# First tile: 64 of each sample's 528 pairs taken ahead, in eight steps of 16 samples, while the other rows are gathered

## What is computed

```python
inner = x[:, row] * x[:, col]                                   # b, 528, 128
fm = relu(einsum('bpd,ad->bpa', inner, attn_W) + attn_b)        # b, 528, 128
scores = einsum('ba,bpa->bp', gnn_feature, fm)                  # b, 528
attn = softmax(scores, axis=1)
attn_output = einsum('bp,bpd->bd', attn, inner) * 100.0         # b, 128
z = concatenate([gnn_feature, attn_output, gnn_feature], axis=1)
y = relu(relu(z @ W_top1 + b_top1) @ W_top2 + b_top2) @ W_top3
```

## Time and profile before

| | us |
|---|---|
| median of 3 runs | 1270.41 |
| the profiled execution, its own time | 1270.63 |
| its span | 1268.2 |
| TensorE busy | 1201.0 |
| VectorE busy | 1147.9 |
| ScalarE busy | 1018.7 |
| POOL busy | 451.8 |

### The profile page before, as it was taken

One profiled execution on the slowest core, in us unless ns is written; L12 is line 12 of the kernel. 1 busy time (PEld: TensorE's weight loads), 2 busy tenths in 40 slices (PEclk: granted clock), 3 DMA queues, 4 the chain that ended last, 5 costly groups with the idle time before them and its releaser, 6 DMA issues.

```text
span 1268.2 us, 20736 instructions
## 1 busy us (share of the span) xinstructions
PE 1201.0 (95%) x8732; PEld 898.7 (71%) x8732; DVE 1147.9 (91%) x649; ACT 1018.7 (80%) x1039; POOL 451.8 (36%) x270
## 2 busy tenths in 40 slices
PE   1499999999999999999999999999999999999998
PEld 1267676777777777777777777677777777777766
DVE  2399899998999989999899989999799998999994
ACT  1288898778987889878897798978888788887883
POOL 6587684018800386005840088201880000000000
PEclk9999999999999999999999999999999999999999
DMA  4211410311103111131101311031110300011001
GB/s 108 97 34 50 105 32 26 102 45 30 34 13 125 31 32 28 30 106 37 32 20 47 106 27 32 20 111 39 30 34 21 117 18 1 1 29 39 17 9 38
DMA packets 54859, 58.83 MB, mean 46 GB/s; under 512 B 10728, under 2 KB 49136, under 8 KB 53744
## 3 DMA queue, kind: packets, MB, share of 16 engines
q1 hardware_dynamic: 46304, 40.20, 10.4%
q0 software_dynamic: 8448, 17.32, 5.2%
q10 hardware_dynamic: 16, 0.00, 0.0%
HBM read 36.12 MB, written 17.31 MB: 42 GB/s over the span
## 4 chain that ended last, share of the span: by engine, by line
PE 83%; ACT 8%; issue 4%; DVE 2%; POOL 2%; another core or an unknown queue 1%; DMA 1%; SPq 0%; ACTq 0%; DVEq 0%; POOLq 0%
PE scores L610 19%; PE ring L580 17%; PE ring L587 13%; PE ring L589 12%; PE ring L588 12%; PE ring L634 4%; ACT fm L308 3%; ACT inner_hi L316 3%; PE ring L620 2%; POOL x_rows L280 2%; PE ring L654 1%; DVE products L418 1%; ACT exp_pairs L323 1%; PE ring L648 1%
## 5 line engine op out<-in xcount | busy, mean ns | idle before, releaser
L308 ACT ACTIVATE fm<-ring,attn_b_sb 128x848 f32<-128x848 f32 (+1 forms) x640 | 597.2, 971 | 183.1 <-PE ring L580 174.3
L418 DVE TENSOR_TENSOR products<-xt 128x2112 f32<-128x2112 f32 x256 | 601.9, 2351 | 37.1 <-ACT xt L347 37.1
L280 POOL DMA_INDIRECT x_rows<-in_tbl,ids_all x264 | 451.1, 1709 | 498.2 <-PE ring L620 408.3
L423 DVE TENSOR_TENSOR low_parts<-products,inner_hi 128x1688 fp32r<-128x1688 f32 (+4 forms) x256 | 467.1, 1825 | 57.1 <-ACT inner_hi L316 56.0
L587 PE MATMUL ring<-inner_hi,attn_wt_lo 128*128 128x424 f32 (+1 forms) x971 | 433.1, 446 | 5.1 <-ACT fm L308 5.1
L316 ACT CAST inner_hi<-products 128x1688 fp32r<-128x1688 f32 (+4 forms) x256 | 392.3, 1532 | 5.2 <-DVE products L418 5.2
L589 PE MATMUL ring<-inner_hi,attn_wt_hi 128*128 128x424 f32 (+1 forms) x971 | 344.1, 354 | 0.0
L588 PE MATMUL ring<-low_parts,attn_wt_hi 128*128 128x424 f32 (+1 forms) x971 | 343.7, 354 | 0.0
L580 PE MATMUL ring<-products,attn_wt 128*128 128x424 f32 (+1 forms) x618 | 275.8, 542 | 10.0 <-issue 6.4
L610 PE MATMUL scores<-fm,gnn_blocks 128*32 128x264 f32 x4096 | 254.6, 389 | 6.5 <-ACT exp_pairs L323 6.4
L587 PEld LDWEIGHTS ring<-inner_hi,attn_wt_lo 128*128 128x128 f32 x971 | 182.6, 188 | 70.8 <-issue 37.6
(11 more groups left out here) (53 smaller groups left out, 203.9 us busy)
## 6 DMA issues: line engine op xcount, KB each, us to landing
x_dram<-x_rows SPq DMA_DIRECT2D x8, 2112.0 KB, 6.6
x_fields<-x_dram SPq DMA_DIRECT2D x128, 128.0 KB
x_rows<-in_tbl,ids_all POOLq DMA_INDIRECT x264
attn_t<-attn_turned SPq DMA_DIRECT2D x124, 32.0 KB, 1.9
w_sb<-in_W_top SPq DMA_DIRECT2D x2, 512.0 KB
x_fields<-in_r_gnn_feature SPq DMA_DIRECT2D x1, 512.0 KB
h<-in_W_top SPq DMA_DIRECT2D x1, 256.0 KB
ids_all<-in_ids SPq DMA_DIRECT2D x1, 132.0 KB, 2.7
```

The source lines that it names most:

```text
L280: nc.gpsimd.indirect_dma_start(out=x_rows[:, f, :], out_offset=None, in_=tables[f], in_offset=bass.IndirectOffsetOnAxis(ap=ids_all[:, t, f ...
L308: nc.scalar.activation(dst, slot(("hidden", pair, j))[:, :, 0:n], ACT.Relu, bias=attn_b_sb[:, 0:1]).then_inc(s_fm, 1)
L418: nc.vector.tensor_tensor(dst, a, b, ALU.mult).then_inc(s_inner, 1)
L423: nc.vector.tensor_tensor(inner[:, S % INNER_BUFS, at:end], plain[:, S % INNER_BUFS, at:end], inner_hi[:, S % HI_BUFS, 0:end - at].bitcast ...
```

## The change

With only the fields 0 to 15 in `xt`, the pairs of a field f in 0 to 7 with the field 1 to 8 further on can be formed: 64 of the 528. The change puts eight steps ahead of step 0, numbered -8 to -1. An ahead step takes 16 samples and their 64 pairs: 1024 columns, two chunks of 512, both native. Its scores take one matmul of 64 columns for each sample, 16 a step, with the same gnn blocks and PSUM places as before. The steps 0 to 31 leave those pairs out: 1856 columns in four chunks of 464 instead of 2112 in five. Their product is two instructions (fields 8 to 32 at distances 1 to 8, 800 columns; all fields at distances 9 to 16, 1056 columns), and half of their score matmuls take 200 columns instead of 264. Steps 0 and 1 have 3 and 2 native chunks. Steps from 32 on are as they were.

The transposes and copies of groups 0 and 1 stay ahead of the loop; those of groups 2, 3 and 4 become jobs of steps -5, -2 and -1, and the two repeats stand behind the relus of steps -7 and -6. product(0) stands on VectorE behind product(-1) and waits for all five copies and the repeats. The rounding of steps 0 and 1 stands behind the jobs of step -1 on ScalarE. The ring's units are now pairs of chunks in order, two chunks a unit, so that an ahead step is one unit and a step of tile 0 two.

```diff
+    AHEAD, AHEAD_SAMPLES = 8, 16
+    BEGIN = -(P // AHEAD_SAMPLES)
+    AHEAD_PAIRS = AHEAD * AHEAD
+    NEAR = AHEAD * (F - AHEAD)
+    LEFT = GROUPS * (PAIRS - AHEAD_PAIRS)
...
-    NATIVE[0], NATIVE[1] = 4, 3
+    NATIVE[0], NATIVE[1] = 3, 2
...
+    def edges(S):
+
+        if S < 0:
+            return list(range(0, AHEAD_SAMPLES * AHEAD_PAIRS + 1, 512))
+        if S < STEPS:
+            return list(range(0, LEFT + 1, LEFT // 4))
+        return EDGES[S % 2]
...
+    FIRST_XT_AT = {-5: 2, -2: 3, -1: 4}
+    FIRST_REPEAT_AT = {-7: 0, -6: 1}
...
-    units = [("x_t", 0, c) for c in range(XJ)]
-    for S in range(ALL):
-        pair, odd = divmod(S, 2)
-        units += [("hidden", pair, j) for j in ((3, 4) if odd else (0, 1, 2))] + jobs_of(S)
+    units = [("x_t", 0, c) for c in range(2)]
+    for S in range(BEGIN, ALL):
+        units += [("hidden", n, 0) for n, pair in enumerate(PAIR_OF) if pair[0][0] == S] + jobs_of(S)
...
         def _(act):
-            def relu(pair, j):
+            def relu(n):
...
-            for c in range(XJ):
+            for c in range(2):
                 evacuate_xt(0, c)
-                if c < K // FU:
-                    repeat(0, c)
-            round_inner(0)
-            round_inner(1)
-            for S in range(ALL):
+            for S in range(BEGIN, ALL):
                 t, s = divmod(S, STEPS)
-                relu(S // 2, 2 if S % 2 else 0)
+                out_now = [n for n, pair in enumerate(PAIR_OF) if pair[1][0] == S]
+                relu(out_now[0])
...
+                if S in FIRST_REPEAT_AT:
+                    repeat(0, FIRST_REPEAT_AT[S])
                 for kind, of, c in jobs_of(S):
...
+                if S == -1:
+                    round_inner(0)
+                    round_inner(1)
...
         def _(dve):
             def product(S):
...
+                if S < 0:
+                    pieces = [((S - BEGIN) * AHEAD_SAMPLES, AHEAD_SAMPLES, 0, AHEAD, 1, AHEAD)]
+                elif S < STEPS:
+                    pieces = [(GROUPS * S, GROUPS, AHEAD, F - AHEAD, 1, AHEAD), (GROUPS * S, GROUPS, 0, F, AHEAD + 1, K - AHEAD)]
+                else:
+                    pieces = [(GROUPS * (S % STEPS), GROUPS, 0, F, 1, K)]
...
-            dve.wait_ge(s_xt_out, XJ)
-            dve.wait_ge(s_repeat, K // FU)
-            product(0)
-            product(1)
-            rest_of_inner(0)
-            product(2)
-            for S in range(ALL):
+            dve.wait_ge(s_xt_out, 2)
+            for S in range(BEGIN, BEGIN + 3):
+                product(S)
+            for S in range(BEGIN, ALL):
...
             def hidden(S):
-                pe.wait_ge(s_inner, S + 1)
-                for c in range(CHUNKS):
+                pe.wait_ge(s_inner, S - BEGIN + 1)
+                for c in range(chunks(S)):
...
-                    if c < NATIVE[S]:
+                    if S < 0 or c < NATIVE[S]:
...
+            def scores_of(S):
+
+                near = [scores[I * j:I * j + I, 0, 0:HALF].rearrange("b (k f) -> b k f", f=F) for j in range(GROUPS)]
+                if S < 0:
+                    for i in range(AHEAD_SAMPLES):
+                        step, j = divmod((S - BEGIN) * AHEAD_SAMPLES + i, GROUPS)
+                        columns = fm[:, S % FM_BUFS, i * AHEAD_PAIRS:(i + 1) * AHEAD_PAIRS]
+                        yield step, j, step == 0, near[j][:, :, 0:AHEAD], columns.rearrange("p (k f) -> p k f", f=AHEAD)
+                    return
+                s = S % STEPS
+                for h in range(2):
+                    for j in range(GROUPS):
+                        if S < STEPS and h == 0:
+                            columns = fm[:, S % FM_BUFS, j * NEAR:(j + 1) * NEAR]
+                            yield s, j, False, near[j][:, :, AHEAD:F], columns.rearrange("p (k f) -> p k f", f=F - AHEAD)
+                            continue
+                        at = j * PAIRS + h * HALF if S >= STEPS else GROUPS * NEAR + j * HALF
+                        yield s, j, s == 0, scores[I * j:I * j + I, h, 0:HALF], fm[:, S % FM_BUFS, at:at + HALF]
...
-            for c in range(XJ):
+            for c in range(2):
                 transpose_x(0, c)
             pe.wait_ge(s_zero, 3)
-            for S in range(ALL):
+            for S in range(BEGIN, ALL):
                 hidden(S)
...
-                if S >= 2 and S % 2 == 0:
+                if S >= BEGIN + 2 and S % 2 == 0:
                     reduce_steps(S - 2)
```

More of the change, by code:

```diff
@@ L69, in jobs_of @@
             jobs.append(("fields", t - 1, FIELDS_AT.index(s)))
-        if s in XT_AT and t + 1 < T:
+        if S in FIRST_XT_AT:
+            jobs.append(("x_t", 0, FIRST_XT_AT[S]))
+        if s in XT_AT and 0 < t + 1 < T:
             jobs.append(("x_t", t + 1, XT_AT.index(s)))
@@ L187, in taken_out @@
             if kind == "hidden":
-                return s_fm, SLOTS * a + b + 1
+                return s_fm, a + 1
             if kind == "fields":
@@ L202, in native_cols @@
         def native_cols(S):
-            return EDGES[S % 2][NATIVE[S]]
+            return edges(S)[NATIVE[S]] if S >= 0 else edges(S)[-1]
         def chunk_place(S, c):
-            pair, odd = divmod(S, 2)
-            j, h = divmod(CHUNKS * odd + c, 2)
-            return slot(("hidden", pair, j)), h
+            return divmod(CHUNK_NO[S, c], 2)
         block = ctx.enter_context(nc.Block())
@@ L383, in _ @@
                     scale_attn(part_at(S, SCALE_AT))
-                relu(S // 2, 3 if S % 2 else 1)
-                if S % 2:
-                    relu(S // 2, 4)
+                for n in out_now[1:]:
+                    relu(n)
+                if S in FIRST_REPEAT_AT:
+                    repeat(0, FIRST_REPEAT_AT[S])
                 for kind, of, c in jobs_of(S):
@@ L599, in reduce_steps @@
                     pe.wait_ge(s_exp, PART_END.index(S0) + 1)
-                if s0 == 0:
-                    pe.wait_ge(s_blocks, t + 1)
-                pe.wait_ge(s_fm, SLOTS * (S0 // 2) + (3 if last_pair else SLOTS))
+                if S0 == BEGIN or s0 == 0:
+                    pe.wait_ge(s_blocks, max(t, 0) + 1)
+                pe.wait_ge(s_fm, relus_by(S0 if last_pair else S0 + 1))
                 for S in (S0, S0 + 1):
                     if last_pair and S > S0:
-                        pe.wait_ge(s_fm, SLOTS * (S0 // 2 + 1))
-                    s = S % STEPS
-                    for h in range(2):
-                        for j in range(GROUPS):
-                            at = j * PAIRS + h * HALF
-                            last = nc.tensor.matmul(scores[I * j:I * j + I, h, 0:HALF], block_of(s, j),
-                                                    fm[:, S % FM_BUFS, at:at + HALF], start=s == 0, stop=s == STEPS - 1,
-                                                    skip_group_check=True)
+                        pe.wait_ge(s_fm, relus_by(S))
+                    for s, j, first, to, columns in scores_of(S):
+                        last = nc.tensor.matmul(to, block_of(s, j), columns, start=first, stop=S % STEPS == STEPS - 1,
+                                                skip_group_check=True)
                 last.then_inc(s_red, 1)
```

82 lines of the change are left out of this document (47 added, 35 removed).

## The result

The changed kernel takes 1308.08 us (median of five runs, 1306.26 to 1311.85) against 1270.41 us (1270.02 to 1271.39, five runs) of the kernel before on the same chip: ratio 1.0294, 95% interval 1.0278 to 1.0311. It is slower by 37.7 us where 9.9 us less were forecast. The profiled execution has span 1309.8 and time 1311.85 us.

What follows compares the result with a forecast made beforehand. TensorE's matmuls were taken to bound the loop, while the front's chain passes through the gathers. Front +3.6 us and rest of tile 0 -13.5 us gave -9.9, from 1270.41 to 1260.5 us; 8-in-10 range 1255 to 1267.5.

Steps and rivals of the forecast that it cites:

- the wait of ScalarE: Old front: 2.5 us between transposes and copy, put down to an unknown queue; charged none, 2.5 us if it came back.
- The ahead start and the walk: Front: TensorE starts ahead work at 30.4 us, step 0 at 59.5, scores of steps 0 and 1 end at 72.9.
- R: Ahead part: time of one pair's 64 score passes of 64 columns, taken as 2.6 us, between 1.3 and 3.84.
- rival (d): Ahead scores: weight loads and passes in line, 0.162 us each, 41.5 us for 256; +31.1 us, 1291.6; chance 0.02.
- Gathers and cover: Ahead part: gathers of tile 0 run 3.2 us later in all, hidden because groups 3 and 4 still land in time.
- rival (a): Join before step 0: a 3.6 us gap brings back the slow clock and R is 3.84; +2.1 + 5.0, 1267.6; chance 0.12.
- The rest of tile 0: Steps 3 to 31 save 10.3 us and fifteen score pairs 3.2, together 13.5; a step takes about 3.65 us.
- (c): Ahead scores: short passes don't overlap and come at 0.129 us each, 33.0 instead of 10.4 us; +22.6, 1283.1; chance 0.07.
- (b): Front: gathers slow to 2.0 us apiece, group 4 lands at 57.1, 1.2 us after it is wanted; 1261.7; chance 0.06.
- (e): Tile 0: ahead work runs but steps don't shorten, because VectorE or the ring sets the step; 1274.0 us; chance 0.03.
- a step 0 after 66 us: End of the front: sign that would make the prediction wrong; step 0's first matmul was forecast near 59.5 us.
- ahead score pairs above 5 us: Ahead part: sign that would make the prediction wrong; a pair was forecast at 2.6 us.

Runs made afterwards that it cites:

- run 7: Kernel before, with a burst of 128 score passes of 264 columns put in beside the gathers of tile 0: 1266.65 us, where the kernel before had 1266.52.
- run 1: Changed kernel with the ahead scores left out but for four matmuls of step -8 and one of each later ahead step: 1263.8 us, ratio 0.9947.
- run 2: Changed kernel with POOL's gathers for tile 1 waiting for the last of the four ahead score pairs: 1270.33 us, ratio 1.0011.
- 13: Kernel before, with a burst of 128 passes of 64 columns and the gathers of tile 0 spaced 1.76 us apart: 1278.78 us.
- run 9: The changed kernel again, unaltered, on a chip where the kernel before took 1267.4 us: 1255.64 us, ratio 0.9906.
- run 10: Kernel before, with a burst of 128 passes of 64 columns beside the gathers of tile 0, on a free chip: 1267.58 us.
- 14: Kernel before, with the burst of 128 short passes and plain SyncE loads replacing the gathers of fields 16 to 32 of tile 0: 1263.48 us.
- 16: Kernel before, with a burst of 128 passes of 264 columns beside the gathers, on a held chip: 1299.28 us.
- 4: Kernel before, with 128 score passes of 64 columns put in behind the transposes of group 1, beside the gathers: 1274.89 us, ratio 1.0035.
- 15: Kernel before, with the burst of 128 passes of 64 columns beside gathers 1.25 us apart, on a held chip: 1276.85 us.

## Why the prediction was wrong

**The step that failed** is the one that let the ahead work stand beside the gathers at the price of its own passes, with "I charge none, and 2.5 us if such a wait comes back on the path" for the wait of ScalarE. That wait was the sign of what decided the result. In the kernel before on a held chip 9 transposes complete 2.5 us late; on a free one it doesn't have the wait (in run 7, the kernel before with a burst that is over by then, the transposes start at 45.82, ScalarE's copy at 47.82 and the first pair of the loop at 64.31, not 67.39), and that is most of the 3 to 4 us between the two sets of its times. I priced it as a constant of the front. It grows with what TensorE does there: 6.1 us for hidden(-4) in run 1, 12.0 us from the 29th pass of the first pair on, and 37.8 us more in the third, when the late join left VectorE idle and so let the gathers of tile 1 run at full pace. The last is a circle: no completion, so no copy and no product; VectorE idle, so gathers 1.25 us apart; so no completion. Before, VectorE is at work from 52.29 us on and the same gathers come 1.4 to 3.4 us apart, and no hold-up is seen. That gathers and pace are needed is shown (2, 13); that VectorE's idleness closes the circle is read from the traces, since no run kept VectorE at work there. Step 0 starts at 112.09 where I had 59.5.

**The ahead start and the walk.** 30.34 us for 30.4. On the free chip step 0 starts at 57.02 and the first pair of tile 0 ends at 70.36 (68.65 + 1.71), for 59.5 and 72.9.

**R, 2.6 us, was mis-sized:** 1.03, below even its lower end of 1.3. That is 0.016 us a pass, near the 0.013 of the columns alone (the 0.053 of the prediction for four); the loads, which I had priced at 0.109 for four, lie beside the passes. Four pairs give 6.3 us back; the cold passes at the start took 1.0 more than I had, the first six passes of step 0 1.4 more. The Trainium skill's rule of rival (d) ("TensorE: Matmul & The Clock Gate", Part 3, The mechanism) is refuted here: 64 loads and 64 passes that span all rows and differ in the column group, in 1.03 us.

**Gathers and cover.** The last gather of tile 0 starts at 48.00 in run 9 for 44.80 before, the 3.2 us of the prediction; group 3 makes TensorE wait 0.18 us. Hidden, as said.

**The clock at the join.** Half of rival (a) came true on the free chip: after 3.57 us of idle TensorE the six passes of step 0 take 3.68 us to the next (57.02 to 60.70), 0.61 each instead of 0.387, and the granted clock is 0.86 in the window of 57 to 69 us. It doesn't happen every time. After the same wait the changed kernel on the held chip takes 4.10 us for them (112.09 to 116.19) at a granted clock of 0.50, and run 1 only 2.62, at 1.00 throughout:
```profile
65.30 2.60 PE L622 MATMUL ring<-products,attn_wt 128*128 128x464 f32 x6 [3.56 <-DVE products L462]
67.92 0.48 PE L629 MATMUL ring<-inner_hi,attn_wt_lo 128*128 128x464 f32 x1
```

**The rest of tile 0.** Pairs are 7.34 us apart ((112.70 - 68.65)/6), 3.67 a step for 3.65, in the held trace too (124.96, 132.22, 139.61); split passes of 464 columns 0.21 us. From the first pair of tile 0 to the last it saves 15.9 us (129.39 in run 10, 113.48 in run 9), for 13.5. The excess lies in the pairs that carry transposes: four take 38.6 us in run 10 and 32.6 in run 9, 6.0 less where four times 0.9 is 3.6. Two of the four take 10.2 us in run 10 and the other two 9.2; the trace shows why, here for the first of the long ones:
```profile
140.45 1.06 PE L620 MATMUL ring<-ident,x_rows 128*128 128x128 f32 x8 [0.78 <-ACT fm L308]
```
TensorE waited there for a bank of the ring. In the changed kernel (run 9) the second transposes, like the other three, come without a wait:
```profile
135.38 1.04 PE L677 MATMUL ring<-ident,x_rows 128*128 128x128 f32 x8
```
I had counted those steps as TensorE's alone. Front +4.1 (64.53 to 68.65), tile 0 -15.9, the rest +0.3: -11.5 between the spans of runs 10 and 9. On the free chip the number comes close (1255.64 lies in the range, at -11.8 us for -9.9), but part of that is luck. The front's 4.1 for 3.6 is two errors that cancel: the new front is 2.5 us shorter than my walk (68.65 for 71.2), and the old one, without its late completion, 2.9 us shorter than the one that I compared with (64.53 for 67.39).

**The rivals.** (c) and (d) had the sign but not the mechanism: their price per pass is nowhere in the trace, and the pairs without gathers beside them refute both. (b) and (e) didn't occur. The threshold "a step 0 after 66 us" did show the failure; "ahead score pairs above 5 us" too (13.0 and 38.8 us).

**What stays open.** What in the chip holds the completions, and what makes a chip held or free. Shown is that it needs POOL's gathers at full pace, not DMA loads as such (14), and not density (1, 16). Every trace comes from an execution under the profiler; the times of the held runs go with their traces (1306 to 1312 us), but every run on record comes with a span and a granted clock, so none shows the kernel without the profiler. Whether its own records take part, which a stop after a nearly fixed number of passes would also fit, was not tested.

## What to carry to other kernels

A wait put down to an unknown queue, on an engine whose releaser had long been done, can be the first sign of a delay that grows, as it was here: before work is moved beside it, ask what it would grow with, and test that before it is priced as a constant. Before TensorE work is put beside gathers at full pace, see to it that it can't feed itself (here: hold the next tile's gathers until the loop runs), since an idle engine may let the disturbance run faster. And an experiment needs its unchanged control beside it on the same chip: four of mine said nothing without it.

## What the runs showed of the hardware

- On a held chip, beside gathers 1.25 us apart, TensorE's completions come late, and it stops 24 to 36 passes into a row of score passes (28 and 24 in the changed kernel, 28 in run 2, 34 in 4, 33 in 15, 36 in 16), which is 40 to 44 with the passes just before; then it goes on in steps of 0.70 us or multiples of it, until 3.2 to 6.4 us behind the last gather's start. At 1.76 us apart only gaps up to 0.42 us are left.
- The same program took 1308.1 us on one chip and 1255.6 on another, where the kernel before differed by 0.3% only.
- 64 short score passes with 64 weight loads in four column groups take 1.03 us, 0.016 us a pass.
- After 3.56 or 3.57 us without a matmul the next six native passes of 464 columns took 3.68 us in run 9 and 4.10 in the changed kernel, but 2.62 in run 1: the slow pace can come back after such a gap, and need not. Before, it was seen after 6.4.
